# The output product in high and low halves: a change to a token tower's kernel on one core

## What is computed

```python
x = emb[ids] * sqrt(256) + pos_enc               # 16 batches of 256 tokens, width 256
q, k, v = x @ w_q, x @ w_k, x @ w_v
o = softmax(q k^T / sqrt(256), axis=queries) v   # attention within a batch, no residual
u = layernorm(o)                                 # norm 1
z, xBC, dt = split((layernorm(u) * ln_w + ln_b) @ in_proj_w.T)   # mixer: width 512, 8 heads
xBC = silu(causal_conv4(xBC) + conv_b)           # xs, B, C
y = ssd(xs * dt, -exp(A_log) * dt, B, C) + D * xs                # chunks of 128 tokens
y = rmsnorm(y * silu(z)) * norm_w
h = o + u + y @ out_proj_w.T                     # the output product of the change
r = layernorm(h)                                 # norm 2
p = softmax(r @ w_router)                        # top 2 of 8 experts, 1024 rows each at most
out = h + bias + sum over top 2: p_e * gelu(r @ w1[e]) @ w2[e]
```

## Time and profile before

| | |
|---|---|
| median of 3 runs | 910.95 us (910.6 to 911.48) |
| profiled execution | 910.75 us, its span 909.0 us |
| TensorE clock granted, mean | 0.996 |
| busy: PE, DVE, ACT, POOL | 888.7, 632.3, 530.6, 507.1 us |

### The profile page before, as it was taken

The page is one execution under the profiler, slowest core; times in us unless marked ns, Lnnn a source line. Parts: engine busy times, 40 slices in busy tenths (PEclk is TensorE's granted clock), DMA queues, the critical chain, the costliest instruction groups (busy, mean ns, idle before and its releaser), DMA issues.

```text
span 909.0 us, 17533 instructions
## 1 busy us (share of the span) xinstructions
PE 888.7 (98%) x5705; PEld 787.8 (87%) x5705; DVE 632.3 (70%) x1708; ACT 530.6 (58%) x1105; POOL 507.1 (56%) x491
## 2 busy tenths in 40 slices
PE   7999999999999999999999889999999999999998
PEld 7888888889888888888788779899999999999997
DVE  1587899889888988898999854646463646464633
ACT  1666777777767777777786654444444444444433
POOL 5656877977887788878866342223223232323243
PEclk9999999999999999999999989999999999999999
DMA  7940111010000000000000107434344334333121
GB/s 221 325 153 13 36 48 35 21 37 24 23 15 22 13 24 12 26 14 23 14 14 4 48 16 227 117 72 110 74 112 76 101 79 94 91 78 60 24 59 47
DMA packets 49381, 59.11 MB, mean 65 GB/s; under 512 B 6288, under 2 KB 44667, under 8 KB 49344
## 3 DMA queue, kind: packets, MB, share of 16 engines
q1 hardware_dynamic: 35904, 42.14, 14.4%
q0 software_dynamic: 13440, 16.50, 10.4%
HBM read 33.62 MB, written 30.67 MB: 71 GB/s over the span
## 4 chain that ended last, share of the span: by engine, by line
PE 81%; DVE 8%; issue 3%; ACT 3%; DMA 2%; POOL 2%; another core or an unknown queue 0%; SPq 0%; DVEq 0%; POOLq 0%; ACTq 0%
PE bank L1659 12%; PE bank L1661 12%; PE bank L1660 12%; PE bank L1721 10%; PE bank L1864 5%; PE bank L1650 5%; PE bank L1832 4%; PE bank L1790 3%; PE bank L1705 3%; PE bank L1696 2%; PE bank L1687 2%; PE bank L1680 2%; DVE xc L1229 2%; DMA w_raw<-w 1%; PE bank L2049 1%
## 5 line engine op out<-in xcount | busy, mean ns | idle before, releaser
L726 POOL DMA_INDIRECT out<-ye,tok_slot x56 | 95.7, 1709 | 229.9 <-DMA out<-ye,tok_slot 117.7
L920 ACT ACTIVATE hf<-bank 128x512 f32<-128x512 f32 x128 | 79.3, 620 | 187.1 <-PE bank L1661 183.1
L1111 DVE TENSOR_TENSOR h_lo<-hf,h_hi 128x512 fp32r<-128x512 f32 x128 | 88.7, 693 | 102.1 <-ACT h_hi L921 100.2
L1229 DVE SCALAR_TENSOR_TENSOR xc<-bank,cw,xc 128x253 f32<-128x253 f32 (+2 forms) x288 | 128.1, 469 | 1.8 <-ACT xc L836 0.2
L1659 PE MATMUL bank<-xe_hi,w_hi 128*128 128x512 f32 x256 | 101.3, 396 | 3.1 <-issue 3.1
L1661 PE MATMUL bank<-xe_hi,w_lo 128*128 128x512 f32 x256 | 101.1, 395 | 0.0
L1660 PE MATMUL bank<-xe_lo,w_hi 128*128 128x512 f32 x256 | 101.0, 394 | 0.0
L663 POOL DMA_INDIRECT slots_dram<-rows,slot x64 | 64.9, 1014 | 58.1 <-DVE slot L1390 27.1
L921 ACT ACTIVATE h_hi<-bank 128x512 fp32r<-128x512 f32 x128 | 79.4, 620 | 0.0
L1659 PE MATMUL bank<-first_w_hi,h_hi 128*128 128x256 f32 x256 | 73.7, 288 | 3.9 <-DVE h_lo L1111 3.9
L1659 PE MATMUL bank<-w_hi,h_hi 128*128 128x256 f32 x256 | 73.0, 285 | 0.0
(11 more groups left out here) (264 smaller groups left out, 2619.4 us busy)
## 6 DMA issues: line engine op xcount, KB each, us to landing
w_raw<-w SPq DMA_DIRECT2D x16, 1024.0 KB
slots_dram<-zero_row SPq DMA_DIRECT2D x1, 8320.0 KB, 29.9
xe<-slots_dram SPq DMA_DIRECT2D x16, 520.0 KB, 4.5
out<-hb SPq DMA_DIRECT2D x16, 256.0 KB, 2.1
w_raw<-in_wT SPq DMA_DIRECT2D x2, 644.0 KB, 4.9
out<-zero_row SPq DMA_DIRECT2D x1, 1024.0 KB, 32.0
slots_dram<-rows,slot POOLq DMA_INDIRECT x64
out<-ye,tok_slot POOLq DMA_INDIRECT x64
```

What stands on the lines that cost most here:

```text
L726: g.indirect_dma_start(out, bass.IndirectOffsetOnAxis(ap=tok_slot[q][:, j:j + 1], axis=0), ye[q][:, j, :], None, compute_op=ALU.add).then_ ...
L920: sc.activation(hf[m % 2][:, :], h_bank[i % H_BANKS][:, :], ACT.Gelu_apprx_tanh).then_inc(hf_ready, 1)
L1111: vc.tensor_tensor(h_lo[:, m, :], hf[m % 2][:, :], h_hi[:, m, :].bitcast(F32), ALU.subtract)\
L1229: ins = vc.scalar_tensor_tensor(out=xc[p][:, m, back:], in0=bank[p][XBC_BANK[i]][:, h * L:(h + 1) * L - back], scalar=cw[:, m, TAPS - 1 - ...
```

## The change

The output product is made in three products by `three`, from `w_out_hi`, `w_out_lo`, `yT` (rounded as ScalarE writes it) and `yT_lo`. GpSimd splits the weight once at the start. VectorE splits yT, chunk by chunk: `split_yT` subtracts the rounded yT from the PSUM bank. TensorE waits for these splits. With this come edits that a sibling of this kernel has: `mask_scores` waits for TensorE's transposes instead of ScalarE's `bs`, and ScalarE's `state_inputs` for gm; norm 2's lm and lv move from the end of a half behind gm of the next (`residual_moments`); the splits of the first expert's second weight (`first_w2_low`) move, two of them into the drain; in the drain VectorE's credits to other engines are given ahead of `last_y`, and a Gelu of one small tile stands on ScalarE behind the router's exponential. Some buffers share memory now (`w_out` raw in y, `below`, `tok_neg`, `across`, `xdec[0]`), for which no instruction is added.

```diff
@@ -576,7 +585,11 @@
 
                 pool.wait_ge(s_wout, 16)
                 pool.wait_ge(s_small, 16 * N_SMALL)
-                g.tensor_tensor(w_out[:, :, :], w_out[:, :, :], bc(nw[:, :].unsqueeze(2), [P, KI, DM]), ALU.mult)\
+                g.tensor_tensor(w_out, w_out, bc(nw[:, :].unsqueeze(2), [P, KI, DM]), ALU.mult).then_inc(w_out_ready, 1)
+                pool.wait_ge(w_out_ready, 1)
+                g.tensor_copy(w_out_hi[:, :, :], w_out).then_inc(w_out_ready, 1)
+                pool.wait_ge(w_out_ready, 2)
+                g.tensor_tensor(w_out_lo[:, :, :], w_out, w_out_hi[:, :, :].bitcast(F32), ALU.subtract)\
                     .then_inc(w_out_ready, 1)
 
             def gather_next(r, p):
...
@@ -857,7 +870,7 @@
                 sc.activation(ea[p][:, :], ea[p][:, :], ACT.Exp)
 
             def state_inputs(r, p):
-                act.wait_ge(btg_psum[p], btg_psum.now(r, p))
+                act.wait_ge(gm_ready[p], gm_ready.now(r, p))
                 sc.activation(bs[p][:, :], bank[p][3][:, 0:NS], ACT.Copy)
                 copy(ea[p][:, :], bank[p][3][:, 3 * P:3 * P + NH], bs_ready[p], ACT.Exp)
 
...
@@ -959,6 +972,7 @@
                     for k in range(KD):
                         sc.activation(xe_hi[0][:, k, :], x_bank[k][:, :], ACT.Copy).then_inc(first_high, 1)
                     router_exp(t, p)
+                    sc.activation(warm[:, :], warm[:, :], ACT.Gelu_apprx_tanh)
                     return
                 if not f:
                     hidden(1, 0)
...
@@ -1250,7 +1264,10 @@
 
                 def mask_scores(r, p, where):
 
-                    dve.wait_ge(bs_ready[p], bs_ready.now(r, p))
+                    if where == p:
+                        dve.wait_ge(btg_psum[p], btg_psum.now(r, p))
+                    else:
+                        dve.wait_ge(bs_ready[p], bs_ready.now(r, p))
                     vc.tensor_tensor(gm[p][:, :, :], bank[where][3][:, P:3 * P].rearrange("p (c l) -> p c l", c=KD),
                                      bc(tri[:, :].unsqueeze(1), [P, KD, P]), ALU.mult).then_inc(gm_ready[p], 1)
 
...
@@ -1307,10 +1324,18 @@
                     vc.tensor_tensor(y[p][:, 0, :], bank[p][YD_BANK[0]][:, :], sz[p][:, 0, :], ALU.mult)\
                         .then_inc(y_ready[p], 1)
                     carried_y(r, p, bank[1 - p][1])
+                    first_w2_low(2)
                     back.wait(carried_y.last)
                     dve.wait_ge(yd_psum[p], yd_psum.now(r, p))
                     own = back.mark(vc.tensor_tensor(y[p][:, 1, :], bank[1 - p][3][:, :], y[p][:, 1, :], ALU.add))
                     gated(r, p, 1, own)
+                    split_yT(r, p, 0, DRAIN_YT)
+
+                def split_yT(r, p, c, banks=YT_BANK):
+                    dve.wait_ge(yT_ready[p], yT_ready.now(r, p, c + 1))
+                    vc.tensor_tensor(yT_lo[p][:, c, :, :].rearrange("p k n -> p (k n)"), bank[p][banks[c]][:, :],
+                                     yT[p][:, c, :, :].rearrange("p k n -> p (k n)").bitcast(F32), ALU.subtract)\
+                        .then_inc(yT_split[p], 1)
 
                 def mean_square(r, p):
                     dve.wait_ge(ss_ready[p], ss_ready.now(r, p))
...
@@ -1327,13 +1352,20 @@
                                                       op0=ALU.mult, op1=ALU.add)
                     ins.then_inc(h2_ready[p], 1)
 
-                def residual_norm(r, p):
+                def residual_stats(r, p):
                     own = Chain(dve, residual_chain, RESIDUAL_LINKS, r, p)
                     hold(dve, h2_ready[p], h2_ready.now(r, p))
                     norm_stats(own, p, h2[p], stats2[p], mv2[p])
+                    own.close()
+
+                def residual_moments(r, p):
+
                     vc.tensor_scalar(lm2[p][:, :], mv2[p][:, :, 0], -1.0, None, ALU.mult)
                     vc.tensor_scalar(lv2[p][:, :], mv2[p][:, :, 1], EPS, None, ALU.add).then_inc(lv2_ready[p], 1)
-                    own.close()
+
+                def residual_norm(r, p):
+                    residual_stats(r, p)
+                    residual_moments(r, p)
 
                 def residual(r, p, where):
                     residual_sum(r, p, where)
...
@@ -1448,8 +1480,14 @@
                     times_dt_early(b, q, 1)
                     with_bias(Turn(PAIRS - 1), q)
                     decay_scores(b, q, 1)
+                    dve.sem_inc(xe_split, 1)
+                    dve.sem_inc(hlo_ready, 2)
+                    dve.sem_inc(ye_ready, 2)
+                    dve.sem_inc(x_half, 2)
                     last_y(b, q)
+                    first_w2_low(3)
                     mean_square(b, q)
+                    split_yT(b, q, 1, DRAIN_YT)
                     first_w1_low(0, 1)
                     first_w1_low(2, 2)
                     for k in range(KD):
...
@@ -1461,10 +1499,6 @@
                     router_in(t, p)
                     residual_norm(b, q)
                     router_top(t, p)
-                    dve.sem_inc(xe_split, 1)
-                    dve.sem_inc(hlo_ready, 2)
-                    dve.sem_inc(ye_ready, 2)
-                    dve.sem_inc(x_half, 2)
                     return
                 if not f:
                     split_h(1, 0)
...
@@ -1485,11 +1519,13 @@
                     return
                 if f:
                     query_max(f, p)
-                if final:
-                    for m in (2 * p, 2 * p + 1):
-                        first_w2_low(m)
                 if b:
                     mask_scores(b, q, q)
+                if f and t:
+                    residual_moments(t, p)
+                if f and final and not p:
+                    first_w2_low(0)
+                    first_w2_low(1)
                 if f:
                     scale_v(f, p)
                 if b:
...
@@ -1516,6 +1552,7 @@
                 if f:
                     split_hT(f, p)
                 if b:
+                    split_yT(b, q, 0)
                     second_y(b, q)
                 if f:
                     dt_in(f, p)
...
@@ -1523,6 +1560,8 @@
                     slots_of(t, p)
                 if nf:
                     embedded(nf, q)
+                if b:
+                    split_yT(b, q, 1)
                 if f:
                     conv(f, p, 0)
                 if t:
...
@@ -1534,7 +1573,8 @@
                 if f:
                     conv(f, p, 2)
                 if b and nf:
-                    residual(b, q, q)
+                    residual_sum(b, q, q)
+                    residual_stats(b, q)
                 if f:
                     front.close()
                 if b:
...
@@ -1858,16 +1898,16 @@
                         .then_inc(yT_psum[p], 1)
 
                 def project_rows(r, p, c, where, ks=range(KI)):
-                    pe.wait_ge(w_out_ready, 1)
-                    pe.wait_ge(yT_ready[p], yT_ready.now(r, p, c + 1))
+                    pe.wait_ge(w_out_ready, 3)
+                    pe.wait_ge(yT_split[p], yT_split.now(r, p, c + 1))
                     for k in ks:
-                        ins = te.matmul(bank[where][0][:, c * DM:(c + 1) * DM], yT[p][:, c, k, :], w_out[:, k, :],
-                                        start=(k == 0), stop=(k == KI - 1))
+                        ins = three(bank[where][0][:, c * DM:(c + 1) * DM], yT[p][:, c, k, :], yT_lo[p][:, c, k, :],
+                                    w_out_hi[:, k, :], w_out_lo[:, k, :], k == 0, k == KI - 1)
                     if c == KD - 1 and ks[-1] == KI - 1:
                         ins.then_inc(out_psum[p], 1)
 
                 def project_out(r, p):
-                    pe.wait_ge(yT_ready[p], yT_ready.now(r, p))
+                    pe.wait_ge(yT_split[p], yT_split.now(r, p))
                     for c in range(KD):
                         project_rows(r, p, c, p)
 
...
@@ -2018,7 +2058,7 @@
                     project_channels(f, p, 0)
                 if nf:
                     if b:
-                        pe.wait_ge(yT_ready[q], yT_ready.now(b, q, 1))
+                        pe.wait_ge(yT_split[q], yT_split.now(b, q, 1))
                     to_xT(nf, q)
                 if f:
                     project_channels(f, p, 1)
```

More of the change, by code:

```diff
@@ L199, in lm_block @@
         mixer = [("xc", [P, MC, L]), ("sz", [P, KD, DI]), ("xs", [P, KD, DI]), ("xdt", [P, KD, DI])]
-        xc, sz, xs, xdt = zip(*[[fb(f"{name}{p}", shape) for name, shape in mixer] for p in range(2)])
+        xc, sz, xs, xdt, yT_lo = [], [], [], [], []
+        for p in range(2):
+            for one, (name, shape) in zip((xc, sz, xs, xdt), mixer):
+                if name == "xdt":
+                    with ExitStack() as own:
+                        yT_lo.append(sb(f"yT_lo{p}", [P, KD, KI, P], F32R, own))
+                one.append(fb(f"{name}{p}", shape))
         tri = fb("tri", [P, P])
-        below = fb("below", [P, P])
         before_b = fb("before_b", [P, P], BF16)
@@ L207, in lm_block @@
```

(20 more changed lines are left out.)

## The result

The changed kernel takes **941.04 us** (median of 4 runs, 940.96 to 941.53) against 911.05 before in the same sessions: ratio 1.0327, 95% interval 1.0312 to 1.0343. It is slower by 30 us. The profiled execution's span is 939.3 us, 30.3 over the 909.0 of before; the granted clock's mean is 0.999.

A forecast was written before the change was run, and what follows sets the result against it. It took a ring from VectorE through ScalarE and GpSimd, as long as TensorE's own work, to bound the kernel. Twelve intervals at +2.3 (27.6), + 2.9 + 1.0 - 1.4 = 30.1 over 910.75 gave 941 us, range 916 to 950.

The forecast's parts named there:

- VectorE's ring: Steady halves: VectorE, ScalarE's softmax and copies, GpSimd's roots, norm 1, y again take 30.84 us, as long as TensorE's work.
- The test on the last body's even half: Kernel before: first_w_lo's extra 1.28 us on VectorE came out as 1.18 in the period, nearly one for one.
- The splits, 1.68 a half: VectorE's two yT splits a batch, with their waits for ScalarE's yT, delay the convolution by 1.68 us.
- shift, 0.6: Norm 1: GpSimd's shift meets VectorE's second seg, takes 1.07 instead of 0.20 us, costing +0.6 a half.
- The moved lm and lv gain 0.6: End of a half: nmax starts 1.33 us earlier, of which 0.6 reaches seg through earlier rows.
- the lock with seg_lo: VectorE's first seg and GpSimd's seg_lo exclude each other; the 0.6 is lost, norm 1's statistics move +0.03.
- TensorE's wait for the splits: Output product: costs nothing, since chunk 0's twelve products (1.43 us) are still ahead of chunk 1's split.
- TensorE idle near 2.9 us a half: Steady halves of the changed kernel: TensorE idles 2.9 us, ahead of the transposes of hn or y.
- rival E: Steady halves: TensorE's 2.9 us idle halves its clock for a microsecond each, 14 us more, 955 us; chance 0.04.
- Last body +2.9: Last body's two halves: even one +1.6, odd one +1.3 as it loses first_w_lo's 1.28; together 2.9 us.
- Start +1: Start: two more GpSimd instructions delay VectorE's small rows in the first batch's chain; +1 us, between 0 and 2 x 1.91.
- Drain -1.4: Drain: earlier credits and Gelu table win up to 3.5 us, splits and first_w_lo cost 2.1; net -1.4.

The follow-up runs named there:

- e4: Changed kernel with both splits still made, but the output product neither uses yT_lo nor awaits the splits; 940.98 us.
- e5: As e4, with VectorE's splits and TensorE's remaining waits for them left out too; 905.78 us.
- e1: Kernel before with all the moves of the change, but a plain output product without halves and splits; 917.22 us.
- f1: Changed kernel with norm 1's shift made by ScalarE instead of GpSimd; 930.00 us.
- e3: Changed kernel with lm and lv back ahead of nmax at the end of the half, the mask's new waits kept; 938.72 us.
- f5: Changed kernel with shift on ScalarE, first split inside second_y, second split behind the convolution's first group; median 941.64 us.
- b1: Kernel before with only the drain edits: credits and Gelu ahead, first_w2_low moved; 905.57 us.
- e2: Changed kernel with lm and lv back ahead of nmax and the mask's two waits as before; median 950.53 us.
- f4: Changed kernel with shift on ScalarE, GpSimd's hb behind the skip rows, lm and lv back, first split inside second_y; 942.25 us.

## Why the prediction was right

**VectorE's ring, not TensorE's own work, sets the end of the changed kernel: right, and shown.** e4 takes work and a wait from TensorE for nothing, e5 takes the splits away for 35 us. The ring goes through TensorE all the same: e1's 0.95 us a half is a wait for TensorE's scores.

**The test on the last body's even half: misread, and its number is luck.** I took its 1.18 us as first_w_lo's 1.28 coming out "nearly one for one". By the rows shown, seg starts at T0+21.90 there (446.65 - 424.75) and at T0+21.98 in a plain half (385.05 - 363.07): VectorE's extra work did not make seg later. It filled the wait of 1.32 us ahead of gm, which is gone in that half. What it did is hold up GpSimd's seg_hi, which took 2.34 us beside it instead of 1.90, in GpSimd's timeline of the kernel before:

```profile
443.20 2.34 POOL L605 TENSOR_TENSOR seg_hi<-tri,a_hi 128x1024 fp32r<-128x1024 f32 x1
```

seg_lo then stood in seg's way. S came 0.54 later behind T0, the next T0 0.64 later behind S, and these two meetings make the 1.18. The splits cost in another way, as the next point shows: they hang on a wait for yT. That extra work on VectorE comes out in the period is shown by e5, not by this half.

**The splits, 1.68 a half, and shift, 0.6: both came out as sized, but they are one mechanism.** Told from T0, the first tap came 1.64 us later (6.52 against 4.88) and the next T0 0.60 later behind S (387.92 - 379.60 = 8.32 against 7.72). The prediction put the two side by side, and e5 shows that both hang on the splits. A late shift makes T0 late against VectorE, and that costs nothing (e5) until an instruction of VectorE waits for something that comes at a fixed distance behind T0. The splits do, for yT: the first has a wait of 0.83 us, where I had counted 0.28, the rest being shift's. f1 takes shift's delay away, gets back 0.75 and stands 1.54 over before.

**The moved lm and lv gain 0.6, and the lock with seg_lo eats it: right in kind, +0.03 was +0.22.** rows waited 0.52 for nm, and seg was caught at 377.79; e3, without the move, is 2.3 us faster, although TensorE has a wait of 1.50 there. Where the other 0.2 comes from stays open.

**TensorE's wait for the splits: the cost was right (none), the reason wrong.** I wrote that chunk 0's products run while chunk 1's split is made. `project_out` waits for both splits. It cost next to nothing because VectorE was just in time: the second split ends at 394.53 and the first product starts at 394.58. In f5 VectorE wasn't, and that wait was 1.70 us.

**TensorE idle near 2.9 us a half, ahead of hn or y: wrong.** It is 1.65 to 1.93, and most of it stands ahead of the segment sums, for ea and seg_lo; 0.43 is ahead of hn and none ahead of y. Some of the missing idle time is tails that count as busy (above); how much of it is not worked out. The sum did not use this figure, rival E did.

**Last body +2.9: it is +2.98, from two misses.** The even half is +1.33 (33.35 - 32.02) where 1.6 was forecast, the odd one +1.65 (32.89 - 31.24) where it was 1.3.

**Start +1: it is +1.95.** One of VectorE's small rows stood for 2.11 us beside GpSimd's w_out_lo, where I had counted two short delays. It is the weight's splitting and not the moves: e1 and b1, without it, have their first T0 at 54.99 and 55.02. Timelines of the changed kernel, and last the same row of the kernel before:

```profile
33.93 2.11 DVE L1210 TENSOR_TENSOR dtq<-dts 128x16 f32<-128x16 f32 x1
...
33.66 2.35 POOL L592 TENSOR_TENSOR w_out_lo<-y,w_out_hi 128x1024 fp32r<-128x1024 f32 x1
...
33.93 0.16 DVE L1196 TENSOR_TENSOR dtq<-dts 128x16 f32<-128x16 f32 x1
```

**Drain -1.4: it is -2.17.** The first expert product comes no sooner against T0 than before (554.39 - 520.48 = 33.91, 521.96 - 488.01 = 33.95), so what the change adds took all the time that the credits won (b1: 518.10 - 487.27 = 30.83, and e5 29.59); but the clock is up, and the 18 products need 3.98 us from first to last start, where they needed 5.57. Together that is 1.63; the other 0.54 lies further on, and no experiment bears on it. b1's drain and experts are 3.96 us shorter, where I had at most 3.5 for the credits: the clock behind the gap was not in my sum.

**Rival E, the clock:** not in the change, where TensorE's idle time of 1.7 to 1.9 us a half is in pieces of 0.80 at most. It is real in kernels a few lines away (e2, f4, f5).

The total came within 0.1 us of 941. That is closer than its terms: start and drain are off by 0.95 and 0.77 in opposite ways.

## What to carry to other kernels

Where several engines go round at one pace, put an extra instruction in by asking what it waits for, and how far behind the pace-setting event that comes: 1.2 us of work cost 2.28 us here, and 0.9 once both waits and shift's delay were out of the way. If a trace has a half in which the engine in question already does extra work, as the last body's here, follow its rows to where the time is lost before its period is taken for the price of such work: here that work went into a wait, and two meetings of VectorE and GpSimd made the longer period.

A wait that is removed in one place tends to come up at the next instruction that hangs on the same event, and a wait in front of TensorE can cost its clock too: in e2's trace the eight products behind one took 3.64 us instead of 1.94. Edits of one kind of stretch, as those of the drain here, are worth timing alone: bundled with the splits they were hidden in a loss, alone they are a gain of 0.7%.

## What the runs showed that was not expected

- The granted clock fell behind single waits of 1.93 (e2) and, in some halves, of 0.75 (f4) and 1.74 (f5), and not behind 1.50 (e3). In f4 and f5 waits of the same length in other halves of the same trace were followed by no fall, so the length of one wait doesn't decide it; what does stays open.
- A tensor instruction of GpSimd and one of VectorE with two SBUF inputs held each other up in both directions, and the small one waited for the large one: VectorE's 128x16 row took 2.11 us instead of 0.16 beside w_out_lo at the start, ohs 1.18 instead of 0.17 beside hb in f4, and GpSimd's 128x4 shift 1.07 instead of 0.20 beside seg.
- One execution of f5 in four took 1235.8 us, at a mean granted clock of 0.653. Its cause is open.
